# Clearing a routing table from another queue, and moving probabilities two periods earlier

## The reference

```python
q, k, v = heads(layernorm(x) @ w_q), heads(ctx @ w_k), heads(ctx @ w_v)
x = x + merge(softmax(q @ k.T * 64 ** -0.5) @ v) @ w_o + b_o
gates = softmax(layernorm(x) @ router_w + router_b)      # [4096, 8]
mask = one_hot(top2(gates)); pos = cumsum(mask) - 1; valid = mask & (pos < 640)
buf[e, pos] = layernorm(x)                               # rows valid for expert e
out = gelu(buf @ w1 + b1) @ w2 + b2
x = x + sum over e of out[e, pos] * gates * valid
```

## Time and profile before

| | us |
|---|---|
| median of 3 runs | 905.82 |
| lowest, highest | 905.12, 907.24 |
| profiled execution | 906.9 |
| its span, first to last instruction | 905.1 |
| TensorE busy in the span | 878.8 (97%) |
| VectorE, ScalarE, GpSimd busy | 725.5, 536.6, 404.4 |
| mean granted clock of TensorE | 0.995 of full speed |

### The profile page before, as it was taken

How to read it: one execution, slowest core, us unless ns; L and a number is a source line. 1 busy time by engine, 2 the same in 40 slices (tenths; PEclk the granted TensorE clock), 3 DMA queues, 4 the chain that set the end, 5 groups by cost and what they waited for, 6 DMA issues and landing times.

```text
span 905.1 us, 21646 instructions
## 1 busy us (share of the span) xinstructions
PE 878.8 (97%) x7552; PEld 779.2 (86%) x7552; DVE 725.5 (80%) x1580; ACT 536.6 (59%) x1535; POOL 404.4 (45%) x622
## 2 busy tenths in 40 slices
PE   7999999999999999999999999999899999999995
PEld 6887888888888888888888888888799999999995
DVE  5667789898979889898898989888888787667861
ACT  5785676676767677676667767666543344234520
POOL 5563435555564654546455464633333312332123
PEclk9999999999999999999999999999999999999998
DMA  8578888888888888878878787877539645664222
GB/s 227 155 217 249 264 246 249 244 247 237 260 236 240 267 244 250 253 241 255 254 236 236 242 247 239 245 220 214 163 109 183 144 91 101 140 136 107 49 28 30
DMA packets 154427, 180.94 MB, mean 200 GB/s; under 512 B 62300, under 2 KB 127946, under 8 KB 150480
## 3 DMA queue, kind: packets, MB, share of 16 engines
q1 hardware_dynamic: 128784, 143.97, 54.2%
q10 hardware_dynamic: 16704, 26.62, 11.2%
q0 software_dynamic: 8832, 8.98, 5.7%
HBM read 106.00 MB, written 78.47 MB: 204 GB/s over the span
## 4 chain that ended last, share of the span: by engine, by line
PE 70%; DVE 11%; DMA 9%; ACT 5%; issue 2%; SPq 1%; POOL 0%; ACTq 0%; POOLq 0%; DVEq 0%
PE psum L816 21%; PE psum L1088 10%; PE psum L1072 10%; PE psum L927 10%; PE psum L883 9%; PE psum L943 7%; DMA squares<-prob 5%; ACT prob L1160 3%; DVE prob L1391 2%; DVE hidl L1308 2%; DMA inverses<-invturned 2%; DVE bufl L1308 1%; PE psum L906 1%; DMA probt<-squares 1%; DVE hidh L1610 1%
## 5 line engine op out<-in xcount | busy, mean ns | idle before, releaser
L1160 ACT ACTIVATE prob<-psum,negmax 128x256 f32<-128x256 f32 x512 | 239.4, 484 | 118.8 <-DVE negmax L1362 103.0
L1362 DVE TENSOR_REDUCE negmax<-psum 128x2 f32<-128x512 f32 x256 | 158.5, 681 | 37.7 <-PE psum L883 37.6
L686 POOL TENSOR_TENSOR al<-attended,ah 128x512 fp32r<-128x512 f32 x57 | 73.8, 1295 | 194.2 <-ACT ah L1099 194.1
L792 POOL DMA_INDIRECT out_rows<-y,rowi x40 | 66.3, 1658 | 159.0 <-DVE y L1620 135.7
L1391 DVE STREAM_TRANSPOSE prob<-prob 128x1024 f32<-128x1024 f32 x116 | 127.6, 1100 | 5.0 <-ACT prob L1160 4.9
L927 PE MATMUL psum<-probt,v 128*64 128x256 f32 x1024 | 124.6, 385 | 1.8 <-DMA probt<-squares 1.8
L1280 ACT ACTIVATE hid<-psum,b1t 128x640 f32<-128x640 f32 x64 | 50.9, 796 | 126.7 <-PE psum L1072 126.7
L1160 ACT ACTIVATION_READ_ACCUMULATOR prob<-psum,negmax 128x1 f32 x512 | 110.2, 215 | 0.0
L927 PEld LDWEIGHTS psum<-probt,v 128*64 128x64 f32 x1024 | 67.9, 136 | 39.1 <-issue 7.2
L1088 PE MATMUL psum<-w2h,hidh 128*128 128x256 f32 x320 | 91.2, 285 | 1.4 <-DVE hidl L1308 1.4
L1088 PE MATMUL psum<-w2l,hidh 128*128 128x256 f32 x320 | 90.5, 283 | 0.0
(11 more groups left out here) (212 smaller groups left out, 2595.0 us busy)
## 6 DMA issues: line engine op xcount, KB each, us to landing
squares<-prob SPq DMA_DIRECT2D x29, 1024.0 KB, 4.9
squares<-prob SPq DMA_DIRECT2D x29, 768.0 KB, 6.3
invrows<-inverses SPq DMA_DIRECT2D x128, 128.0 KB
probt<-squares SPq DMA_DIRECT2D x58, 256.0 KB, 4.8
probt<-squares ACTq DMA_DIRECT2D x58, 256.0 KB, 6.0
probt<-squares SPq DMA_DIRECT2D x58, 192.0 KB, 3.7
probt<-squares ACTq DMA_DIRECT2D x58, 192.0 KB, 4.3
w1r<-in_w SPq DMA_DIRECT2D x8, 1024.0 KB, 5.3
```

The costliest lines, as they stand in the source:

```text
L686: pool.tensor_tensor(al[:, b % 2, c:c + 2, :], attended[:, :, :], ah[:, b % 2, c:c + 2, :].bitcast(F32), ALU.subtract).then_inc(sem("a_lo" ...
L792: pool.indirect_dma_start(out=out_rows, out_offset=bass.IndirectOffsetOnAxis(ap=rowi[:, e % 2, s:s + 1], axis=0), in_=y[:, e % 2, s, :], i ...
L1160: last = act.activation(into, out_of, ACT.Exp, bias=negmax[:, m % 2, u, qb:qb + 1], accum_out=total[:, m % 2, u, qb:qb + 1])
L1362: dve.tensor_reduce(negmax[:, m % 2, u, :], psum[:, u, :].rearrange("p (q s) -> p q s", q=ST), AX.X, ALU.max, negate=True).then_inc(sem("m ...
```

## The change

Four things are edited. `MOVED` begins at period 2 instead of 4. `clear` is now ScalarE's: two halves of four experts in periods 1 and 2, each one DMA, in which a partition writes five rows of an expert as one run of 5300 bytes (before: 128 rows of one run each, five times); the second half is followed by the spare rows. `constants` is done in period 0, before the second context, on GpSimd. And the spare rows' numbers in `blank` are laid out to match. The waits for the cleared table count two DMAs in place of eight.

```diff
-MOVED = range(4, PERIODS - 2)
+MOVED = range(2, PERIODS - 2)
...
-    out += [*steps("q q_hi", 1), ("vsplit", 0), ("ctx", 1), ...
+    out += [*steps("q q_hi", 1), ("vsplit", 0), ("constants", 0), ("ctx", 1), ...
...
         if four:
-            out += steps("exp0 exp1", m) + ([("a_hi", m - 2)] if m >= 2 else []) + [("q_hi", m + 1)]
+            out += steps("exp0 exp1", m) + [("clear", m - 1)] + ([("a_hi", m - 2)] if m >= 2 else [])
+            out += [("q_hi", m + 1)]
...
             out += [("q_lo", m + 1), ("square0", m), ("k_lo", m + 1), ("square1", m), ("a_norm", m - 2)]
+            out += [("a_lo", m - 2)] if m - 2 < POOL_REST[0] else []
...
-        out += {1: [("vsplit", 1)], 2: [("constants", 0)], 3: ...
+        out += {1: [("vsplit", 1)], 3: ...
...
-        out += {2: steps("clear", 0), 3: steps("clear", 1), 4: steps("clear", 2)}.get(m, [])
...
-            def clear(third):
-                sp.wait_ge(sem("blank"), 1)
-                for e in range(3 * third, min(3 * third + 3, NE)):
-                    sp.dma_start(table[e * CAP:(e + 1) * CAP, :].rearrange("(s p) w -> p s w", p=P),
-                                 blank[:, :, :]).then_inc(sem("table_clear"), 16)
-                if third == 2:
-                    sp.dma_start(out_rows[N:N + CAP, :].rearrange("(s p) w -> p s w", p=P),
-                                 blank[:, :, 0:D]).then_inc(sem("spare_clear"), 16)
...
-                    pool.wait_ge(sem("table_clear"), 16 * NE)
+                    pool.wait_ge(sem("table_clear"), 16 * 2)
...
-                link(pool.iota(dumpi[:, :], pattern=[[P, ET]], base=N, channel_multiplier=1))
+                link(pool.iota(dumpi[:, :], pattern=[[1, ET]], base=N, channel_multiplier=ET))
...
+            def clear(half):
+                act.wait_ge(sem("blank"), 1)
+                count = NE // 2
+                rows_of = table[half * count * CAP:(half + 1) * count * CAP, :]
+                act.dma_start(rows_of.rearrange("(e p s) w -> p e s w", e=count, p=P),
+                              blank[:, :, :].unsqueeze(1).to_broadcast([P, count, ET, ROW]))\
+                   .then_inc(sem("table_clear"), 16)
+                if half == 1:
+                    act.dma_start(out_rows[N:N + CAP, :].rearrange("(p s) w -> p s w", p=P),
+                                  blank[:, :, 0:D]).then_inc(sem("spare_clear"), 16)
```

More of the change, by code:

```diff
@@ L103, in timeline @@
     out += steps("split_hi split_lo", 2) + steps("split_hi split_lo", 3) + steps(q, 0) + steps(k, 0)
-    out += [*steps("q q_hi", 1), ("vsplit", 0), ("ctx", 1), *steps("scores max0 max1 exp0", 0), ("q_lo", 1),
+    out += [*steps("q q_hi", 1), ("vsplit", 0), ("constants", 0), ("ctx", 1), *steps("scores max0 max1 exp0", 0), ("q_lo", 1),
             *steps("max2 max3", 0), ("split_hi", 4), *steps(k, 1), ("exp1", 0), ("split_lo", 4),
@@ L173, in timeline @@
         out += [("ctx", b + 1)] if r == 2 and 1 <= b < B - 1 else []
-        out += {1: [("vsplit", 1)], 2: [("constants", 0)], 3: [("residual", 0), ("residual", 1)], 4: [("vsplit", 2)],
+        out += {1: [("vsplit", 1)], 3: [("residual", 0), ("residual", 1)], 4: [("vsplit", 2)],
                 5: [("vsplit", 3)]}.get(m, [])
@@ L590, in load_base @@
                   .then_inc(sem("base_in"), 16)
-            steps = dict(load_ctx=load_ctx, clear=clear, inv_out=inv_out, inv_in=inv_in, lift=lift, move_low=move_low, traffic=traffic,
+            steps = dict(load_ctx=load_ctx, inv_out=inv_out, inv_in=inv_in, lift=lift, move_low=move_low, traffic=traffic,
                          load_w=load_w, load_base=load_base)
@@ L1248, in _ @@
             steps = dict(split_hi=split, xt_hi=xt, q_hi=q, k_hi=k, v_sb=v_, a_hi=pv, x2t_sb=x2t_, gate_exp=gate,
-                         x2t_part_sb=x2t_part, ln2=ln2, scale=scale, row_hi=row_hi, gelu_table=gelu_table, move_high=move_high,
+                         x2t_part_sb=x2t_part, ln2=ln2, scale=scale, clear=clear, row_hi=row_hi, gelu_table=gelu_table, move_high=move_high,
                          w_hi=lambda piece: split_w(0, piece),
```

## The result

The changed kernel took 911.5 us (median of 22 runs), the kernel before 907.15 us beside it (22 runs): ratio 1.0041, 95% interval 1.0031 to 1.0052. It is slower by 0.4%, where 901.7 us (899.2 to 905.2 us) was forecast. The profiled execution took 912.65 us with a span of 910.9 us; that of the kernel before had 905.1 us. Each ratio in this document is estimated over all executions, so it need not equal that of the two medians; one execution of the kernel before beside g1_moved_from_three (1207.62 us, granted clock 0.654) is left out.

What follows compares the result with a forecast made beforehand. TensorE, busy 97% of the span, was taken as the bound, with time to win before 80 us. The terms -4.22 - 1.82 + 0.3 + 0.9 + 0.5 + 0.2 = -4.1 us gave 901.7 us from 905.82 us, range 899.2 to 905.2 us.

Steps and rivals of the forecast that it cites:

- What shares the engines: Period 0's inverses, written and read back beside the first clear: normalisation slips by nothing to about 3 us, 0.3 us taken.
- The rule that was weighed: Queues share 16 engines and interleave: period 2's lift gets half during the clear, 3.7 us instead of 1.8 us.
- a clock under 1.00: Sign of being wrong: a granted clock under 1.00 after 26 us; no size was given.
- "small transfers" rival: Read of period 0's inverses lands 3 us late, period 2 grows by about 2.6 us: 904.0 us, chance 0.14.
- Period 3: TensorE's matmul stream without turned heads becomes like period 7: 8.13 us, -2.04 us.
- Period 4: TensorE's matmul stream becomes like period 7 without its turn: 7.69 us, -2.18 us.
- Pace of periods 3 and 4: VectorE, and the exps behind it, may pace these two periods: 0.5 us lost (bounds 0 and 1.5).
- VectorE in period 2: Two block transposes come in, 1.23 and 0.69 us; scores of period 3 start about 0.6 us later.
- The stall at 75 us: TensorE's wait for moved probabilities, whose moves shared the engines with clears, goes: -1.82 us.
- ScalarE's issues: First clear issue free, period 2's two about 2 x 0.8 us; 0.9 us taken together with VectorE's transposes.
- The first lift and move: Period 2's lift takes 7 us beside the second clear, move lands before pv(2): 0.2 us (bounds 0 and 1.5).
- slower, the first move stands behind the second clear: ScalarE's half of the first move queues behind the second clear, pv(2) waits 11 us: 911 us, chance 0.08.

Runs made afterwards that it cites:

- g1_moved_from_three: Changed kernel with probabilities moved from period 3 on and SyncE clearing two, three, then three experts with the spare rows: 909.64 us, ratio 0.9972 to the kernel before.
- e8_same_queue: Changed kernel with the same two halves of the clear and the spare rows issued by SyncE instead of ScalarE: 906.67 us, ratio 0.9985 to the kernel before.
- e4_busy_wait: Changed kernel in which TensorE computes k(3) six times over where it would otherwise stand: 916.93 us, ratio 1.0069 to the kernel before.
- e1_moved_only: Kernel before with only the moved periods beginning at 2, clears and constants where they were: 921.24 us, ratio 1.0109 to the kernel before.
- f1_three: Changed kernel with SyncE clearing in three pieces (two, four, two experts), the last with the spare rows ahead of the first lift: 905.07 us, ratio 0.9983.
- f2_last_behind_read: As f1_three, but the last piece is issued behind the first lift and the read of inverses(1): 904.51 us, ratio 0.9980 to the kernel before.
- e5_after_again: The changed kernel as it is, run again on the second chip: 913.01 us, ratio 1.0045 to the kernel before.
- e2_clears_only: Changed kernel with the moved periods beginning at 4 again, the clears staying early on ScalarE: 920.34 us, ratio 1.0093 to the kernel before.
- e6_second_late: Changed kernel with the second half of the clear and the spare rows issued by ScalarE in period 3: 915.37 us, ratio 1.0077 to the kernel before.
- e7_spread: Changed kernel with one clear DMA per expert, spread over periods 1 to 4 on ScalarE, spare rows in period 5: 910.67 us, ratio 1.0030.
- f3_three_unmoved: As f1_three, but the first moved period is 4 as in the kernel before: 910.13 us, ratio 1.0046 to the kernel before.
- e3_short_pieces: Changed kernel with each half cleared by four DMAs of one expert in 1060 B pieces: 918.61 us, ratio 1.0077 to the kernel before.

## Why the prediction was wrong

**The step that failed is "What shares the engines".** It took 0.3 us for the read of the inverses, with 0 and about 3 us as its ends. Measured, the normalisation slipped by 8.9 us: 4.2 us on the write and the rest on the read, and period 2 grew by 10.9 us. Three things in it were wrong. First, it let only the first half of the clear meet the inverses. The second half met the read too, since it was issued at 31.64 us instead of 34 us and the write held the read's issue back to 32.29 us. Second, the reason for the low end, "here nothing stands ahead of it in its own queue": an empty queue of its own did not help the read, with the second half issued 0.65 us ahead of it in ScalarE's. With that half issued behind it and in its own queue it took 2.95 us (e8_same_queue). Third, the size: the far end was a row in which a write stood behind other transfers (6.9 us), and it was applied to the pair as a whole. The two transfers are in series, each met a clear of its own, and each could be late by as long as a clear lasts: 10.4 us from issue to landing. That bound could have been worked out from the forecast's own terms, since it had the first half draining until 33.5 us and the second from 36 to 45 us.

**The rule that was weighed.** The runs agree with the Trainium skill, "DMA: Bandwidth & Descriptors", section "Issuing engines are not separate DMA queues", in that another queue brought no way around the 16 engines. But interleaving did not mean an even share by queue: at half of about 400 GB/s the read's two transfers of 128 KB would take 1.3 us, and the read took 9.7 us. The prediction applied the rule to the lift, which in the changed kernel met no clear at all (47.90 to 51.95 us), and not to the transfers that TensorE waits for first.

**The granted clock was not in the sum.** A wait of 7 us of TensorE in period 2 took the clock to 1.2 GHz until 54.7 us: period 3 gained 0.25 us instead of 2.04. With the clock up (e4_busy_wait) period 3 gained all of it, but period 4 lost 1.3 us, so the clock's own price is 0.4 to 1.2 us of the 5.6 lost. The prediction named a clock under 1.00 as a sign of being wrong, but no rival was charged for it; the "small transfers" rival, 904.0 us, had the right mechanism with a third of its size.

**What was right.** Period 3: 8.12 to 8.13 us in four kernels that move from period 2 and have the clock at 1.00 there (e1_moved_only, e4_busy_wait, f1_three, f2_last_behind_read). Period 4: -2.18 us, to the hundredth, but with luck: it took 7.69 us where TensorE had been slow in period 3, and 8.00 us in e5_after_again. No run has both periods at their forecast lengths; together they took 17.61 us in the changed kernel, 16.72 us in e5_after_again and 17.13 us in e4_busy_wait, against 15.82 + 0.5 us forecast. So the term "Pace of periods 3 and 4" was of the right kind and rather too small: 1.3 us in e4_busy_wait, where its range was 0 to 1.5. VectorE in period 2: 0.6 us forecast for the transposes, 0.60 us in e1_moved_only. The stall at 75 us: -1.88 against -1.82 us. ScalarE's issues: 0.40 us for the first, 0.37 and 1.09 us for the two of period 2, about the 2 x 0.8 us taken; in the changed kernel they are hidden behind the late inverses. The first lift and move: no wait of TensorE in the changed kernel, but only because everything came 10 us later and the clear was over. What they would have cost at 40.5 us beside the second half is not shown; f1_three, where a lift issued at 39.48 us beside another last clear took 10.1 us instead of the 7 us allowed, suggests more than 0.2 us. The constants cost nothing that can be seen. The rival "slower, the first move stands behind the second clear" gave the right sign and time (911 us) by a mechanism that did not act: the wait was for the inverses, ahead of it.

Not forecast: period 1 is 1.0 us shorter, since the granted clock stayed at 1.00 between 22 and 25.6 us, where the kernel before had 0.54 and 0.61.

## What to carry to other kernels

Before a long transfer is moved, list every small transfer on the critical path that is issued or in flight while it drains, on any queue, and take the rest of the drain as the upper bound for each; two in series can each pay. Take the long transfer's place from when its issue can run, not from the instruction ahead of it in the list. Another queue did not protect a small transfer here. Issuing the small one first and the long one behind it in the same queue did: the read took 2.95 us with 2.7 MB behind it (e8_same_queue, f2_last_behind_read) and 9.7 us with them issued ahead. And count the bytes: 5.4 MB of clears at 410 GB/s are 13 us of full engines, which fit between two small transfers only in pieces, and none of these runs found a free place for the last piece beside the first lifts. Last, a period that TensorE can run faster is not faster until the engines that feed it are: here VectorE took back over 1 us of the gain of two moved periods in a row.

## What the runs showed that was not expected

- A 16 KB write took 5.6 to 6.5 us and a read of two times 128 KB 9.3 to 10.2 us beside 2.7 MB of another queue issued ahead of them (changed kernel, e2_clears_only, e4_busy_wait, e5_after_again; e6_second_late for the write). With no clear ahead of it still in flight the read took 3.0 to 4.3 us (e6_second_late, e7_spread, e8_same_queue, f2_last_behind_read). With 1060 B rows instead of 5300 B pieces it was not much better: 7.8 and 6.4 us.
- The clock in period 1: TensorE's waits before scores at 19.8 and 21.5 us are the same 0.97 and 0.76 us to within 0.02 us in all kernels; the profiles of the three kernels that move from period 4 (before, e2_clears_only, f3_three_unmoved) show a clock of 0.50 to 0.73 from 22 to 26 us and scores of period 2 at 30.2 to 30.3 us, those of the kernels that move earlier 1.00 and, e3_short_pieces aside, scores at 29.1 to 29.4 us. This 1 us goes with the moved range and not with the clears (e1_moved_only has it, e2_clears_only does not); its cause stays open.
